# Splitting each expert's weight load in two, and moving the shared down weights into the tokens' place

## The reference, cut to what matters

```python
gu = x @ se_gate_up_w.T                                  # shared expert, 2 x 1408 wide
shared = silu(gu[:, :I_sh]) * gu[:, I_sh:] @ se_down_w.T
shared = shared * sigmoid(x @ shared_gate_w.T)
probs = softmax(x @ gate_w.T)                            # 60 experts
weights, sel = top_k(probs, 4)
for each of the 60 experts:                              # I = 352
    gu_e = x @ w13_e.T                                   # 512 -> 704
    h = silu(gu_e[:, :I]) * gu_e[:, I:]
    acc = acc + cw_e[:, None] * (h @ w2_e.T)             # 352 -> 512
x = x + shared + acc
```

## Time and profile before

| | |
|---|---|
| time, median of 3 runs | 1194.88 us (1192.4 to 1199.11) |
| the profiled execution's own time | 1196.25 us |
| its span in the trace | 1194.2 us |
| mean granted TensorE clock | 0.972 |
| TensorE busy | 1100.5 us, 92% of the span |
| DMA | 233.15 MB, 195 GB/s over the span |

### The profile page before, as it was taken

The page is one execution under the profiler, slowest core; times in us unless marked ns, Lnnn a source line. Parts: engine busy times, 40 slices in busy tenths (PEclk is TensorE's granted clock), DMA queues, the critical chain, the costliest instruction groups (busy, mean ns, idle before and its releaser), DMA issues.

```text
span 1194.2 us, 18726 instructions
## 1 busy us (share of the span) xinstructions
PE 1100.5 (92%) x5550; PEld 592.8 (50%) x5550; DVE 505.7 (42%) x1385; ACT 263.5 (22%) x806; POOL 367.1 (31%) x843
## 2 busy tenths in 40 slices
PE   3999799998999989999989999999998989998797
PEld 1444465445644455544655555554544444444354
DVE  7843574339644485535746701222121111211144
ACT  0322242323333332323414010111111111111000
POOL 3575451856437472574100370000000000000252
PEclk9999799999999989999999999999999989989899
DMA  9999201000010000102013984999999999999643
GB/s 315 320 397 382 99 2 55 15 1 13 12 46 15 13 2 23 46 3 95 1 42 105 380 300 160 373 381 379 373 381 375 387 382 386 385 394 353 181 130 109
DMA packets 76587, 233.15 MB, mean 195 GB/s; under 512 B 11362, under 2 KB 13766, under 8 KB 68814
## 3 DMA queue, kind: packets, MB, share of 16 engines
q1 hardware_dynamic: 58830, 197.90, 45.7%
q10 hardware_dynamic: 11520, 20.98, 5.0%
q0 software_dynamic: 6144, 13.13, 3.7%
HBM read 178.75 MB, written 53.22 MB: 194 GB/s over the span
## 4 chain that ended last, share of the span: by engine, by line
PE 66%; DMA 10%; DVE 9%; SPq 8%; issue 4%; ACT 1%; DVEq 0%; ACTq 0%
PE ps L833 14%; PE ps L917 7%; PE ps L1201 7%; PE ps L1118 6%; PE ps L1197 6%; DMA arena<-in_w 6%; SPq L472 6%; PE ps L1300 5%; PE ps L1233 3%; PE ps L1229 3%; DMA arena<-in_se_down 2%; PE ps L1175 2%; PE ps L974 2%; DMA arena<-in_x 1%; PE ps L906 1%
## 5 line engine op out<-in xcount | busy, mean ns | idle before, releaser
L833 PE MATMUL ps<-arena 128*100 128x512 f32 (+3 forms) x576 | 223.6, 535 | 5.6 <-ACT arena L1322 3.7
L767 POOL DMA_INDIRECT arena<-ys_d,slot_u x32 | 33.2, 1037 | 426.6 <-issue 417.5
L833 PEld LDWEIGHTS ps<-arena 128*100 128x100 f32 (+1 forms) x576 | 88.4, 176 | 102.5 <-issue 92.4
L1201 PE MATMUL ps<-arena 128*64 128x352 f32 x640 | 111.7, 507 | 20.8 <-DMA arena<-in_w 12.2
L2048 DVE COPY arena<-ps 128x512 f32<-128x512 f32 x40 | 27.7, 692 | 223.9 <-PE ps L1189 223.9
L917 PE MATMUL ps<-arena 128*100 128x512 f32 x256 | 114.1, 593 | 0.0
L1118 PE MATMUL ps<-arena 128*128 128x400 f32 x288 | 98.3, 501 | 2.3 <-DVE arena L2028 1.1
L1197 PE MATMUL ps<-arena 128*128 128x352 f32 x320 | 98.1, 459 | 0.8 <-issue 0.8
L1374 ACT ACTIVATE arena<-ps,arena 100x345 f32<-100x345 f32 x128 | 69.5, 547 | 111.9 <-DVE arena L1819 109.3
L1201 PEld LDWEIGHTS ps<-arena 128*64 128x64 f32 x640 | 50.6, 150 | 77.0 <-issue 66.8
L693 POOL TENSOR_TENSOR arena<-arena 115x512 f32<-115x512 f32 (+1 forms) x29 | 30.5, 1051 | 163.1 <-DVE arena L1746 125.9
(11 more groups left out here) (227 smaller groups left out, 1520.2 us busy)
## 6 DMA issues: line engine op xcount, KB each, us to landing
arena<-in_w SPq DMA_DIRECT2D x60, 1408.0 KB, 11.4
arena<-in_w SPq DMA_DIRECT2D x60, 512.0 KB, 12.4
xs_d<-zero SPq DMA_DIRECT2D x5, 3328.0 KB, 25.4
arena<-in_w SPq DMA_DIRECT2D x60, 192.0 KB, 13.5
arena<-xs_d ACTq DMA_DIRECT2D x40, 256.0 KB, 7.5
ys_d<-arena ACTq DMA_DIRECT2D x40, 256.0 KB, 7.4
ys_d<-zero SPq DMA_DIRECT2D x2, 3328.0 KB, 25.6
arena<-in_se_up SPq DMA_DIRECT2D x11, 512.0 KB, 6.5
```

What stands on the lines that cost most here:

```text
L833: last = nc.tensor.matmul(ps[0:m, k, 0:cols[1] - cols[0]], lhs(c), w[:, c, cols[0]:cols[1]], start=(c == 0), stop=(c == n_c - 1))
L1201: last = nc.tensor.matmul(ps[half * HALF:(half + 1) * HALF, 3 + gu, 0:I], xsT[1][:, c, half * HALF:(half + 1) * HALF], w13_s[s][1 + half][ ...
```

## The change

Each expert's load is cut into its first weights (`load_w13`) and its second (`load_w2`), each with a signal of its own. `gate_up` now waits for the first alone, and `down` has a wait for the second. The refill (`refill`) sends each part when the product that read the place before is done: the pair's w13 of round i + 2 after the pair's first product of round i, the single's w2 after its second product, the w13 of the next round's single after that single's first product, and the pair's w2 after the pair's second product. `w_down` changes places with `acc` and `dnT`: it now stands where the tokens were, and is sent right after the last expert's weights, while `acc` is loaded into slot set 0 after both second products of round 18.

```diff
-        acc = carve(B, D)
-        dnT = carve(DC, 400)
+        w_down = carve(MC, D)
         assert top[0] <= xT3_end
...
         top[0] = down_at
-        w_down = carve(MC, D)
+        acc = carve(B, D)
+        dnT = carve(DC, 400)
...
+            def load_w13(s, b, at):
+                e = sp.value_load(pos_i[0:1, bass.ds(at, 1)], min_val=0, max_val=E - 1)
+                sp.dma_start(w13_s[s][b], w13[e, :, :, :]).then_inc(w13_ready[s][b], 16)
+
+            def load_w2(s, b, at):
+                e = sp.value_load(pos_i[0:1, bass.ds(at, 1)], min_val=0, max_val=E - 1)
+                sp.dma_start(w2_s[s][b][:, 0:2, :], w2[e, 0:256, :]...).then_inc(w2_ready[s][b], 16)
+                sp.dma_start(w2_s[s][b][0:96, 2, :], w2[e, 256:I, :]).then_inc(w2_ready[s][b], 16)
...
+            def refill(s, i, last=False):
+                sp.wait_ge(gu_full[1], i + 2)
+                sp.sem_inc(load_gate, 1)
+                for n in range(2):
+                    load_w13(s, 1 + n, (i + 2) * 2 + (SINGLES + n))
+                sp.wait_ge(y_full[0], i + 2)
+                sp.sem_inc(load_gate, 1)
+                load_w2(s, 0, i + 2)
+                if not last:
+                    sp.wait_ge(gu_full[0], i + 3)
+                    sp.sem_inc(load_gate, 1)
+                    load_w13(1 - s, 0, i + 3)
+                sp.wait_ge(y_full[1], i + 2)
+                sp.sem_inc(load_gate, 1)
+                for n in range(2):
+                    load_w2(s, 1 + n, (i + 2) * 2 + (SINGLES + n))
...
             load_expert(1, 2, 2 + SINGLES + 1)
-            with sp.Fori(0, ROUNDS // 2 - 1) as ii:
+            sp.wait_ge(gu_full[0], 2)
+            load_w13(0, 0, 2)
+            with sp.Fori(0, ROUNDS // 2 - 2) as ii:
                 for s in range(2):
-                    sp.wait_ge(y_full[0], ii * 2 + (s + 2))
-                    sp.sem_inc(load_gate, 1)
-                    load_single(s, ii * 2 + (s + 2))
-                    sp.wait_ge(y_full[1], ii * 2 + (s + 2))
-                    sp.sem_inc(load_gate, 1)
-                    load_pair(s, ii * 2 + (s + 2))
+                    refill(s, ii * 2 + s)
+            refill(0, ROUNDS - 4)
+            refill(1, ROUNDS - 3, True)

             sp.wait_ge(sh_up, UNITS)
-            sp.dma_start(acc[0:S], x2_d.rearrange("b s d -> s b d")).then_inc(acc_loaded, 16)
+            sp.dma_start(w_down, se_down.rearrange("(c p) n -> p c n", p=P)).then_inc(down_loaded, 16)
             sp.wait_ge(y_full[0], ROUNDS)
             sp.wait_ge(y_full[1], ROUNDS)
-            sp.dma_start(w_down, se_down.rearrange("(c p) n -> p c n", p=P)).then_inc(down_loaded, 16)
+            sp.dma_start(acc[0:S], x2_d.rearrange("b s d -> s b d")).then_inc(acc_loaded, 16)
...
             def gate_up(k, s, turn, j):
                 for b in ((0,), (1, 2))[k]:
-                    pe.wait_ge(w_ready[s][b], j * 48 + 48)
+                    pe.wait_ge(w13_ready[s][b], j * 16 + 16)
...
-            def down(k, s, turn):
+            def down(k, s, turn, j):
+                for b in ((0,), (1, 2))[k]:
+                    pe.wait_ge(w2_ready[s][b], j * 32 + 32)
```

More of the change, by code:

```diff
@@ L375, in decoder_kernel @@
         perm_ready = sem("perm_ready")
-        w_ready = [[sem(f"expert{s}{b}_loaded") for b in range(3)] for s in range(2)]
+        w13_ready = [[sem(f"expert{s}{b}_up_loaded") for b in range(3)] for s in range(2)]
+        w2_ready = [[sem(f"expert{s}{b}_down_loaded") for b in range(3)] for s in range(2)]
         xs_loaded = [[sem(f"xs_loaded{k}{s}") for s in range(2)] for k in range(2)]
@@ L541, in _ @@
             sp.dma_start(xn3[0:S], xn3_d.rearrange("b s d -> s b d")).then_inc(xn3_loaded, 16)
-            def load_expert(s, b, at):
[L544 to L554, removed]
+            def load_w13(s, b, at):
[3 more added lines that the diff above has]
+                e = sp.value_load(pos_i[0:1, bass.ds(at, 1)], min_val=0, max_val=E - 1)
+                sp.dma_start(w2_s[s][b][:, 0:2, :], w2[e, 0:256, :].rearrange("(p c) n -> p c n", c=2)).then_inc(w2_ready[s][b], 16)
+                sp.dma_start(w2_s[s][b][0:96, 2, :], w2[e, 256:I, :]).then_inc(w2_ready[s][b], 16)
+            def load_expert(s, b, at):
+                load_w13(s, b, at)
+                load_w2(s, b, at)
+            def refill(s, i, last=False):
[14 more added lines that the diff above has]
+                    load_w2(s, 1 + n, (i + 2) * 2 + (SINGLES + n))
             for m in range(3, 6):
@@ L558, in _ @@
             sp.wait_ge(perm_ready, 1)
-            load_single(0, 0)
+            load_expert(0, 0, 0)
             load_expert(0, 1, SINGLES)
@@ L562, in _ @@
             load_up(6)
-            load_single(1, 1)
+            load_expert(1, 0, 1)
             load_up(7)
@@ L1246, in round_ @@
                 transpose_rows(0, 1 - s, i + 1, next_j)
-                down(0, s, i)
+                down(0, s, i, j)
                 transpose_hidden(1, i)
@@ L1250, in round_ @@
                 transpose_rows(1, 1 - s, i + 1, next_j)
-                down(1, s, i)
+                down(1, s, i, j)
                 transpose_hidden(0, i + 1)
@@ L1266, in _ @@
             gate_up(1, 1, ROUNDS - 1, last_j)
-            down(0, 1, ROUNDS - 1)
+            down(0, 1, ROUNDS - 1, last_j)
             transpose_hidden(1, ROUNDS - 1, False)
-            down(1, 1, ROUNDS - 1)
+            down(1, 1, ROUNDS - 1, last_j)
             pe.wait_ge(y_ready[0], ROUNDS + 1)
```

## The result

Over 16 runs of each kernel the median went from 1199.34 us to 1182.24 us; the ratio is 0.987 with a 95% interval of 0.9846 to 0.9893, that is 12.8 to 18.5 us less. (Runs that took over 1.5% longer than the fastest of their kernel are left out of the ratios.) The forecast was 20.6 us less and 1175 us: the direction and most of the mechanism were right, the gain by the ratio is about three quarters of what was worked out. The time lies just above the forecast's own range of 1169 to 1181 us, beside the 1183 us of rivals A and B, and inside the whole range. Part of that lies with the kernel before: its median over 16 runs is 4.5 us above the 1194.88 us of three runs that the sum started from. The profiled execution took 1185.29 us, its span 1183.3 us.

The account below looks back on a forecast made before the run. From 748 us the DMA weight stream was taken as the bound. 8.7 us from its start and 11.9 from the tail, 20.6 off the profiled 1196.25, and 1.4 for the median gave 1174.3, called 1175; own range 1169 to 1181, whole 1168 to 1185.

Parts of the forecast that it names:

- A: Tail: shared second product starts 16 us after the last expert lands, not 8.2; gain 12.8, 1183 us; chance 0.09.
- B: Start of the stream: parts sent early give nothing; gain 11.9, 1183 us; chance 0.07.
- What bounds it: Expert stage: from 748 us the weight stream's bytes set the end; in the last twelve rounds by 2.7 us a round.
- Earlier refills: Start of the expert stage: filling the DMA hole recovers 8.7 us, bounds 5 to 12.
- The rate: Weight stream: 387 GB/s taken where TensorE stalls, 378 where unbroken; 1.4 us left to the range.
- The last round and `w_down`: Tail: experts' work and `w_down` both done at 1102.9, the latter 8.2 us after the last expert; 11.9 us gained.
- The weighed rule: Tail: `acc` held ten engines back ahead of `w_down`; behind it `w_down` runs at full rate, otherwise 3.5 us dearer.
- More instructions: Rounds: three more TensorE waits a round and more expert-number reads on SP cost nothing; at most 2.5 us a round.
- `acc` last: Tail: later `acc` moves VectorE's first addition 5.6 us later against the shared product, inside its first wait; costs nothing.
- After L1320's start: From the shared second product's start to the end: 70.7 us, unchanged.
- C: Refill stream slows to 358 GB/s throughout: 24 us lost against 20.6 won, 1198 us; chance 0.07.
- D: TensorE's clock: slow first products make rounds 21.6 us, 25 us lost against 20.6 won, 1200.5 us; chance 0.03.

Follow-up runs that it names:

- mixed kernel: The change with early refills for the first eight and late refills from round 10 on, against the kernel before: 1186.0 us, ratio 0.9859.
- few transfers under way: The change, with SP waiting ahead of each part until an earlier one landed: 1183.9 us, 0.9893; with `w_down` in four parts too: 1178.4 us, 0.9861.
- late order: The change with refills waiting as long as in the kernel before, new places and part order kept: 1187.6 and 1190.7 us, ratios 0.9875 and 0.9922.
- exchange alone: The kernel before with only the places and the two transfers of `w_down` and `acc` exchanged: 1191.1 us, ratio 0.9935.
- split alone: The change's split loads and early refills, with the old places and `w_down` sent behind `acc`, against the kernel before: 1197.4 us, ratio 0.998.

## Why the prediction was right, and what it mis-sized

*What bounds it* held: in every trace the DMA share is 1.02 or 1.03 from 760 us to 1060 us, and TensorE waits in the late rounds.

*Earlier refills* is the step that was mis-sized: the ratios give 4.6 us for them (about 0.5 to 9) where the sum had 11.2 (8.7, and 2.5 for the single's second weights moving behind). Adding up the stretches from the stage's start gives the lead in bytes. The kernel before, from 725.15 us:

```profile
725.15:735.15 10.00, 8.72 (x33) 5.30 (x35) 1.80 (x5) 0.50 (x2) 0.00 (x0) 1.00 0.77 270
735.15:745.15 10.00, 10.00 (x52) 5.20 (x51) 1.80 (x5) 1.53 (x3) 0.00 (x0) 1.00 0.16 45
745.15:755.15 10.00, 10.00 (x44) 5.02 (x44) 2.32 (x6) 1.06 (x2) 0.00 (x0) 1.00 0.95 325
755.15:765.15 10.00, 10.00 (x52) 5.30 (x49) 1.86 (x6) 1.06 (x2) 0.00 (x0) 1.00 1.01 393
```

And the change, from 723.15 us:

```profile
723.15:733.15 10.00, 8.72 (x33) 5.30 (x35) 1.80 (x5) 0.51 (x2) 0.00 (x0) 1.00 0.99 350
733.15:743.15 10.00, 10.00 (x52) 5.20 (x51) 1.80 (x5) 1.52 (x3) 0.00 (x0) 1.00 0.52 191
743.15:753.15 10.00, 10.00 (x44) 5.02 (x44) 2.33 (x6) 1.06 (x2) 0.00 (x0) 1.00 1.01 396
753.15:763.15 10.00, 10.00 (x52) 5.29 (x49) 1.84 (x6) 1.06 (x2) 0.00 (x0) 1.00 1.03 375
```

After these 40 us it is 13.1 MB in the trace of the change and 10.3 in both of the kernel before: 2.8 MB, 7.4 us at 378 GB/s, as forecast but for 1.3 us of idle time more. Then part of it melts: between 40 and 160 us the kernels with early refills carry 44.2 to 44.6 MB in nine traces, those with late refills 44.9 to 46.0 in five. From 160 to 360 us both kinds carry the same on the mean, 75 MB, and scatter from 74 to 77. After 360 us the means are 132.7 and 130.9 MB (without the mixed kernel), 1.8 MB or 4.8 us, with single traces from 131.9 to 134.0 and from 129.5 to 132.8. The sentence that failed is that every landing moves by 8.7 us because the stream "needs what it needed". Why the early ones run some 2% slower in rounds 2 to 7 is open. The two kinds stand apart most clearly from 760 to 820 us, 372 to 376 GB/s against 377 to 384. The kernels with few transfers under way belong to the lower kind there (373 and 375), but they don't rule out the depth: in that stretch their first weights landed 10.1 and 10.3 us after the issue, beside 11.1 in the change and 7.9 to 9.2 with late refills. That the pair's second weights now stand next to each other is not enough of a reason: they do so in the late order too, which carried 46.0 and 45.2 MB.

*The rate.* 387 GB/s was one execution's. In its other trace the kernel before has 378 from 920 to 1060 us instead of 386, and the change has 370 to 382. One per cent of the rate is 3.5 us, so a sum made from one trace of a stage bounded by bytes carries, by estimate, some 5 us of the run in it. In the profiled execution this is most of the miss: L1320 389.3 us after the stage's start instead of 377.8; of those 11.5 us, 8.2 are 310 us at 372.6 GB/s instead of 382.6 (40 to 350 us; some 2 of them belong to rounds 2 to 7 and so to the change), 1.3 the smaller lead, 2.1 the tail. These two executions are 11.0 us apart where the medians are 17.1 apart: the one before was faster than its median and the one after slower, so this account overstates the miss.

*The last round and `w_down`* held in kind. Last second weights were no longer waited for, the pair's product ran at the full clock (4.95 us for 7.87); from its start to L1320 were 16.6 us instead of 14.5; in between the engines moved 316 GB/s at a share of 0.96, and not 387. The exchange alone gave 7.8 us for the 5.6, the order of the pair's parts about 3, give or take 5, for the 3.8. The split with early refills and the exchange give 2.4 and 7.8 us alone and about 15.4 together.

*The weighed rule* (the Trainium skill, "DMA: Bandwidth & Descriptors", "Why a DMA increments its semaphore by 16 and not by 1": a transfer over 100 partitions is spread over 10 of the 16 engines) agrees with the trace in its direction. In the change, from 1112 to 1116 us, `w_down` has landed and `acc` is still on its way: the DMA share is 0.65 at 227 GB/s, and ten of sixteen are 0.63. With `acc` behind, `w_down` went at nearly the full rate, 384 GB/s; with `acc` ahead, in the split alone, 213 GB/s passed. But the share was 1.05 there, so all sixteen count as busy, which ten engines do not explain. The tail of the split alone is 11.4 us longer than the change's, more than the 7 us that `acc` would need on the ten engines that the Trainium skill names there, an estimate at the rate of 387 GB/s; what the rest is, no run shows.

*More instructions* cost nothing that shows: rounds 0 to 7 of the change still take 19.45 us (19.44 from 730.22 to 749.66, its first two `late_up`). *`acc` last* ate 7.17 us of VectorE's first wait and 2 of its second instead of 5.6 of the first, still nothing at the end. *After L1320's start* 70.8 us for 70.7.

*The rivals.* A, the long tail, is what happens with the split alone, not with the change. B is refuted by the lead of 2.8 MB, yet half true: a lead is not kept whole. C was real in size, a rate 1 to 4% lower. By the sign that the prediction set for it, under 375 GB/s in the last twelve rounds, C would stand in three of the change's four traces; but the exchange alone (373) and the late order (374 and 370) meet that sign too, so it mostly tells of the run, and the size of C's own part is open. D did not come: slow products (6.6 us or more) in five of the change's last eight rounds, inside the slack. The stalls began three rounds later, as said.

## What to carry to other kernels

Where bytes are the bound, ask first when the stream begins and what stands behind its last byte, and do both: here an earlier stream gave nothing measurable while the tail's transfer stood behind another. Order the last transfers by who waits for them, and send what nobody waits for last. Take the rate from several executions before a sum is built on it.

## What the runs showed of the hardware

The same kernel's stream carried 370 to 382 GB/s in the late rounds of four executions at the same DMA share of 1.03, and nothing in the stretches that I read explains it. SP's issue instructions for weights, 0.34 us otherwise, lasted up to 6.2 us once some 9 MB were under way (an estimate: 25 us to landing at 372 GB/s), and up to 8.4 us for `acc`; the kernel with few transfers under way has no long weight issues and the same time, so no cost of that shows. Transfers on ACT's queue landed in 9 us even then, beside 7.8 in the kernel before, while SP's first weights took 27: a deep queue on one engine held up the other's by about 1 us. A transfer over 100 partitions, `acc`, left the DMA share at 0.65 to 0.66 and 196 to 232 GB/s when it came last, in the four traces of the change and in the kernel with few transfers under way.
